# Rotary layers with one projection and an exchange of halves, and a first stage without added base rows

## What is computed

```python
for _ in range(3):
    prev = slots
    q = _ln(slots, lnq_g, lnq_b) @ wq + bq
    attn = softmax(k·q / scale, over the slots) + EPS_ATTN, each slot's share normalised over the tokens
    upd = jnp.einsum('bnk,bnd->bkd', attn, v)
    slots = upd @ wu + bu + prev
    h = _ln(slots, lnm_g, lnm_b) @ w1 + b1
    slots = gelu(h) @ w2 + b2 + slots
    slots = _ln(slots + x_cls[:, None, :], lnp_g, lnp_b)
```

```python
x1, x2 = (x[..., :half], x[..., half:])
return jnp.concatenate([x1 * cos - x2 * sin, x1 * sin + x2 * cos], axis=-1)
```

## Time and profile before

| | |
|---|---|
| median of three runs | 3954.4 us |
| the profiled execution, its own time | 3957.59 us |
| its span, first to last instruction | 3955.8 us |
| granted TensorE clock, mean | 0.963 |
| busy: TensorE, VectorE, ScalarE, GpSimd | 89%, 63%, 57%, 36% |
| stage "6", from the first context matmul at 2030.5 us to the end of its last layer and "7" | about 1925 us |

### The profile page before, as it was taken

One profiled execution on the slowest core, in us unless ns is written; L12 is line 12 of the kernel. 1 busy time (PEld: TensorE's weight loads), 2 busy tenths in 40 slices (PEclk: granted clock), 3 DMA queues, 4 the chain that ended last, 5 costly groups with the idle time before them and its releaser, 6 DMA issues.

```text
span 3955.8 us, 59358 instructions
## 1 busy us (share of the span) xinstructions
PE 3527.9 (89%) x23199; PEld 1634.4 (41%) x23199; DVE 2478.4 (63%) x4794; ACT 2263.7 (57%) x3266; POOL 1420.6 (36%) x1419
## 2 busy tenths in 40 slices
PE   6877999998899999989977898989999999989988
PEld 5667344443734444435551233333333333333334
DVE  6653544444365445534658787778877778778844
ACT  5524554553255555544314666677677777767784
POOL 5543433434244213420022243443443443443412
PEclk8889999999999999999987999999999999999998
DMA  3021100000210110011111011110110110110100
GB/s 124 12 69 56 50 17 23 6 17 25 78 40 23 28 34 6 23 46 35 33 44 49 11 47 28 44 50 26 44 50 26 44 50 26 52 42 26 41 12 17
DMA packets 139226, 146.05 MB, mean 37 GB/s; under 512 B 37241, under 2 KB 120649, under 8 KB 137238
## 3 DMA queue, kind: packets, MB, share of 16 engines
q1 hardware_dynamic: 135876, 135.96, 11.7%
q0 software_dynamic: 3072, 6.30, 0.5%
HBM read 69.00 MB, written 12.59 MB: 21 GB/s over the span
## 4 chain that ended last, share of the span: by engine, by line
PE 58%; DVE 24%; ACT 7%; POOL 6%; issue 3%; DMA 2%; SPq 1%; DVEq 0%; POOLq 0%; ACTq 0%
PE ps L1997 7%; PE ps L2013 6%; PE ps L2208 5%; DVE c1sm L2974 5%; DVE c0sm L2974 4%; PE ps L2125 3%; PE ps L2045 3%; PE ps L2194 2%; PE ps L2152 2%; PE ps L1938 2%; PE ps L2244 2%; PE ps L2252 2%; PE ps L1880 2%; ACT wA L2457 2%; PE ps L1870 2%
## 5 line engine op out<-in xcount | busy, mean ns | idle before, releaser
L2457 ACT ACTIVATE wA<-ps 128x1024 f32<-128x1024 f32 (+1 forms) x574 | 575.6, 1023 | 209.7 <-PE ps L2194 205.4
L2974 DVE TENSOR_REDUCE c0sm<-ps 128x2 f32<-128x1024 f32 x384 | 455.0, 1219 | 99.9 <-PE ps L2152 97.3
L2974 DVE TENSOR_REDUCE c1sm<-ps 128x2 f32<-128x1024 f32 x384 | 454.3, 1218 | 82.1 <-PE ps L2152 80.1
L2749 DVE TENSOR_REDUCE c1sm<-ps 128x2 f32<-128x1024 f32 x128 | 153.0, 1220 | 182.5 <-PE ps L1962 180.0
L2457 ACT ACTIVATE wB<-ps 128x1024 f32<-128x1024 f32 (+1 forms) x194 | 198.5, 1023 | 63.8 <-PE ps L2194 62.1
L2457 ACT ACTIVATE c0m<-ps 128x1024 f32<-128x1024 f32 (+1 forms) x192 | 196.2, 1022 | 59.0 <-PE ps L2194 57.3
L2749 DVE TENSOR_REDUCE c0sm<-ps 128x2 f32<-128x1024 f32 x128 | 151.9, 1219 | 93.9 <-PE ps L1962 92.3
L1734 PE MATMUL ps<-CST 128*128 128x256 bf16 x1330 | 190.4, 296 | 10.4 <-DMA CST<-in_cst 7.9
L3111 POOL TENSOR_SCALAR c0sm<-c0sm 128x4 f32<-128x4 f32 x40 | 7.8, 196 | 517.4 <-DVE c0sm L2529 517.0
L3111 POOL TENSOR_SCALAR c1sm<-c1sm 128x4 f32<-128x4 f32 x40 | 7.9, 196 | 509.8 <-DVE c1sm L2529 509.2
L2194 PE MATMUL ps<-c0ar 64*128 64x512 bf16 (+1 forms) x864 | 164.9, 388 | 25.2 <-DVE c1sm L2974 11.2
(11 more groups left out here) (980 smaller groups left out, 8366.6 us busy)
## 6 DMA issues: line engine op xcount, KB each, us to landing
c0ar<-c0m SPq DMA_DIRECT2D x216, 128.0 KB, 2.5
c1ar<-c0m SPq DMA_DIRECT2D x216, 128.0 KB, 2.4
c0m<-rscr SPq DMA_DIRECT2D x96, 128.0 KB, 3.0
c1m<-rscr SPq DMA_DIRECT2D x96, 128.0 KB, 3.0
wA<-in_x SPq DMA_DIRECT2D x1, 4112.0 KB, 21.6
wA<-in_x SPq DMA_DIRECT2D x1, 4096.0 KB, 12.9
wA<-in_lay SPq DMA_DIRECT2D x3, 1346.0 KB, 5.8
wB<-in_lay SPq DMA_DIRECT2D x3, 1346.0 KB, 5.8
```

The costliest lines, as they stand in the source:

```text
L2457: e.activation(P.ap[0:n, :, :], u.ap[0:n, :].rearrange("p (a q) -> p a q", a=2), ACT.Exp, scale=S8).then_inc(*A(("P8", n0, s, k), free=[u]))
L2749: e.tensor_reduce(c.sm[:, 2 * (g % 2), 2 * j:2 * j + 2], u.ap.rearrange("p (h k) -> p h k", h=2)[:, :, 0:n], AX, ALU.max, negate=True).the ...
L2974: e.tensor_reduce(c.mneg[:, j, :, s // 4, s % 4], u.ap.rearrange("p (a k) -> p a k", a=2), AX, ALU.max, negate=True).then_inc(*V(free=[u]))
```

## The change

The rotary weights are stored once. TensorE makes one projection into one bank, VectorE multiplies it by the cosine rows and by the sine rows (reading the same bank twice), and four DMAs of 32 partitions each exchange the halves of the sine product, since the halves of a head lie 32 partitions apart. GpSimd adds the exchanged product and goes on as before. A buffer `R` has 1536 columns in place of 1280, a layer's packed weights have 512 columns fewer.

In the first stage `s0base` is gone. The bias `bu` is added to the context's value rows once for each batch, before the rounds (the shares of a slot sum to one, so it comes out as a bias). `BC` is put into PSUM by an identity matmul ahead of the second one, and VectorE adds `y` itself.

The planner's constants and seeds of stages "0", "1", "2" and "6" are other ones; those of "3", "4" and "5" are the same. The costs in the requests follow the new steps.

```diff
-    "6": dict(lag=0.0744, weight=0.0116, even=0.0008, held=0.2624, table=1.1605, apart=55.0617, spread=0.0027, seed=2100, stagger=13.3148, ...
+    "6": dict(lag=0.0395, weight=0.0032, even=0.0016, held=0.2624, table=1.3751, apart=55.0617, spread=0, seed=7767, stagger=13.3148, ...
...
-        R6 = Bufs([carve(1280) for _ in range(3)])
+        R6 = Bufs([carve(1536) for _ in range(3)])
...
-                yield from do("s0base", c, ("base", k), w["bu"], chain=[("G", 1.3)], after=t)
...
-                yield from do("s0base", c, ("base2", k), BC[:, 128 * b:128 * b + 128], chain=[("G", 1.3)], after=ty)
...
-            (U, R), t = yield Want([("T", 1.92 * ncol / 512), ("V", 2.2 * ncol / 1024 + .12), ("G", 1.3)], [two, R6], t)
-            emit("rp", ch, n, ww, src, skey, ncol, U, R)
-            two.give(U, t[1])
-            t = t[2]
+            (U, R), t = yield Want([("T", 0.96 * ncol / 512), ("V", 2.2 * ncol / 1024 + .12)], [banks, R6], t)
+            emit("rp", n, ww, src, skey, ncol, U, R)
+            banks.give(U, t[1])
+            _, t = yield Want([("S", 1.3)], after=t[1])
+            emit("rx", ch, n, ncol, R)
+            _, t = yield Want([("G", 1.3)], after=t[0])
+            emit("rpa", ch, n, ncol, R)
+            t = t[0]
...
+            def rx(ch, n, ncol, R):
+                w.wait_ge(*V.at(("rp", n)))
+                for p in range(0, 128, 32):
+                    q = p ^ 32
+                    e.dma_start(R.ap[p:p + 32, 1024:1024 + ncol], R.ap[q:q + 32, 512:512 + ncol]).then_inc(*D("x" + ch)(("rx", n)))
...
-            def s0w2(c, k, h, u):
+            def s0w2(c, b, k, h, u):
+                w.wait_ge(*V.at("bc"))
+                for s in u.clear():
+                    w.wait_ge(*s)
+                e.matmul(u.ap, IDN, bc4(BC[:, 128 * b:128 * b + 128]), start=True, stop=False, skip_group_check=True)
                 w.wait_ge(*A.at(("s0h", k)))
-                for s in u.clear():
-                    w.wait_ge(*s)
                 for j in range(4):
-                    i = e.matmul(j4(u.ap, j), j4(h.ap, j), W0["w2"], start=True, stop=True)
+                    i = e.matmul(j4(u.ap, j), j4(h.ap, j), W0["w2"], start=False, stop=True, skip_group_check=True)
...
-                for k in range(2):
-                    i = e.matmul(U.ap[:, 512 * k:512 * k + ncol], j4(ww, k), src, start=True, stop=True)
-                i.then_inc(*T(("rp", n)))
+                e.matmul(U.ap[:, 0:ncol], ww, src, start=True, stop=True).then_inc(*T(("rp", n)))
...
-                w.wait_ge(*G.at(("base2", k)))
-                e.tensor_tensor(c.y, v4(u.ap), v4(c.ar[:, 1700:2212]), ALU.add).then_inc(*V(free=[u]))
+                w.wait_ge(*V.now())
+                e.tensor_tensor(c.y, v4(u.ap), c.y, ALU.add).then_inc(*V(free=[u]))
...
-                    e.tensor_tensor(o, v, CSIN, ALU.mult).then_inc(*V(("rp", n), free=[U]))
+                    e.tensor_tensor(o, bcg(U.ap, 2), CSIN, ALU.mult).then_inc(*V(("rp", n), free=[U]))
...
-            def rp(ch, n, ww, src, skey, ncol, U, R):
+            def rpa(ch, n, ncol, R):
                 o = R.ap
-                w.wait_ge(*V.at(("rp", n)))
-                e.tensor_tensor(o[:, 0:ncol], o[:, 0:ncol], o[:, 512:512 + ncol], ALU.add).then_inc(*G(("rp", n)))
+                w.wait_ge(*D("x" + ch).at(("rx", n)))
+                e.tensor_tensor(o[:, 0:ncol], o[:, 0:ncol], o[:, 1024:1024 + ncol], ALU.add).then_inc(*G(("rp", n)))
...
-LAY_COLS = [(n, 256) for n in ("q", "k", "cq", "ck")] + [(n, 128) for n in ("v", "so", "cv", "co")] + \
+LAY_COLS = [(n, 128) for n in ("q", "k", "cq", "ck", "v", "so", "cv", "co")] + \
```

More of the change, by code:

```diff
@@ L32 @@
     "5": dict(lag=0.0459, weight=0.0146, even=0.0061, held=0.012, table=3.6948, apart=0, spread=0.3107, seed=2311, bias=dict(G=0.872, TVA=-0.769, TAV=0.748, S=0.899, VG=-1.033, TV=0.596, T=1.359, V=-1.043, TA=0.476, TVAV=0.305, VTA=0.117), turns=(), shift=-24.819, keep=0.0),
-    "6": dict(lag=0.0744, weight=0.0116, even=0.0008, held=0.2624, table=1.1605, apart=55.0617, spread=0.0027, seed=2100, stagger=13.3148, bias=dict(T=0.244, S=0.373, VTA=-0.191, TVb=-0.054, A=-0.534, VG=-0.949, G=-0.49, TA=-0.046, TAb=-0.043, TAV=0.203, TVAV=0.587, TVV=0.107, V=0.182), turns=((13, 247, 0.3), (53, 150, 0.0), (379, 276, 0.3), (419, 456, 0.0), (3849, 853, 0), (3874, 642, 1.0), (4746, 100, 0), )),
+    "6": dict(lag=0.0395, weight=0.0032, even=0.0016, held=0.2624, table=1.3751, apart=55.0617, spread=0, seed=7767, stagger=13.3148, bias=dict(T=0.244, S=-0.259, VTA=-0.191, TVb=-0.054, A=-0.534, VG=-0.932, G=-0.369, TA=-0.046, TAb=-0.043, TAV=0.203, TVAV=0.253, TVV=0.107, V=-0.062, TVG=0.358, TVA=0.238), turns=((53, 150, 0.0), (419, 456, 0.0), )),
 }
@@ L733, in stage0 @@
                 c.zT.give(zt, t[0])
[L734 to L735 removed]
+                (u,), t = yield Want([("T", .95), ("V", .69)], [banks], t[1])
+                emit("s0w2", c, b, k, h, u)
                 banks.give(u, t[1])
@@ L1709, in store @@
                 e.dma_start(o[:, b], xb(b)).then_inc(*D("st_o")("o"))
-            run(dict(load=load, pre=pre, zl=zl, w1b=w1b, ysd=ysd, lay0=lay0, lay=lay, lay7=lay7, i6m=i6m, rd=rd, md=md, mw=mw, rq=rq, rw=rw, rb=rb, out=store))
+            run(dict(load=load, pre=pre, zl=zl, w1b=w1b, ysd=ysd, lay0=lay0, lay=lay, lay7=lay7, i6m=i6m, rx=rx, rd=rd, md=md, mw=mw, rq=rq, rw=rw, rb=rb, out=store))
             w.wait_ge(*D("st_o").at("o"))
@@ L2561, in s0c @@
                 e.memset(vw[:, 128:129], 1.0).then_inc(*V())
-                e.tensor_copy(vw[:, 0:128], u.ap[0:NCTX, 0:128]).then_inc(*V())
+                e.tensor_tensor(vw[:, 0:128], u.ap[0:NCTX, 0:128], W0["bu"][0:NCTX, :], ALU.add).then_inc(*V())
                 e.tensor_scalar(c.sm[0:NCTX, 0, 0:1], u.ap[0:NCTX, 128:129], S128, None, ALU.mult
@@ L2595, in s0u @@
                 r2 = c.sm[:, 6, 0:4]
-                base = v4(c.ar[:, 1700:2212])
-                w.wait_ge(*G.at(("base", k)))
+                w.wait_ge(*V.now())
                 for h, p in enumerate((u, u2)):
@@ L2605, in s0u, with s0w2 @@
                         i = e.scalar_tensor_tensor(out=c.y[:, q, :], in0=pv_[:, j, 0:128], scalar=r2[:, q:q + 1],
-                                                   in1=base[:, q, :], op0=ALU.mult, op1=ALU.add)
+                                                   in1=c.y[:, q, :], op0=ALU.mult, op1=ALU.add)
                     i.then_inc(*V(free=[p]))
-            def s0w2(c, k, h, u):
+            def s0w2(c, b, k, h, u):
                 w.wait_ge(*T.at(("s0w2", k)))
-                w.wait_ge(*G.at(("base2", k)))
-                e.tensor_tensor(c.y, v4(u.ap), v4(c.ar[:, 1700:2212]), ALU.add).then_inc(*V(free=[u]))
+                w.wait_ge(*V.now())
+                e.tensor_tensor(c.y, v4(u.ap), c.y, ALU.add).then_inc(*V(free=[u]))
             def xadd(c, b, dep=None):
@@ L3125, in lnb @@
                 e.tensor_tensor(c.ve, c.ve, c.rs, ALU.mult).then_inc(*G(("rs", n)))
-            def s0base(c, key, row):
-                base = v4(c.ar[:, 1700:2212])
-                w.wait_ge(*V.at("bc"))
-                e.tensor_tensor(base, c.y, bc4(row), ALU.add).then_inc(*G(key))
             def en(u):
@@ L3336, in arrays_of @@
     perm = np.array([(2 * s + p) * 8 + dd for p in range(2) for dd in range(8) for s in range(8)])
-    twin = np.array([(2 * s + p) * 8 + (dd + 4) % 8 for p in range(2) for dd in range(8) for s in range(8)])
     turn = np.array([(8 * q + 4 * y + i) * 8 + dd for q in range(2) for i in range(4) for y in range(2) for dd in range(8)])
-    both = lambda w: np.concatenate([w[:, perm], w[:, twin]], axis=1)
     lays = []
```

23 lines of the change are left out of this document (11 added, 12 removed).

## The result

The changed kernel takes 3950.7 us in the median of 19 runs (3937.2 to 3957.2), the kernel before 3958.4 us in 19 runs beside it. The ratio is 0.9979 with a 95% interval of 0.9970 to 0.9987. So it is faster by 0.2%, 8 us (5 to 12), where 28 us were forecast.

What follows compares the result with a forecast made beforehand. TensorE was taken to lead stage "6" at 91% busy, with VectorE a second limit close by. Terms -39 + 16 - 5 = -28 us gave 3929.6 us, stated as 3926 us against the median; range 3885 to 3968.

Steps and rivals of the forecast that it cites:

- more than a dozen exchanges: Sign of a wrong prediction: the chain shows more than a dozen exchanges; two to six were expected in stage "6"'s body.
- The rotary matmuls, -39: Stage "6", TensorE: one projection fewer per rotary step frees 65 us, of which 0.6 comes back, -39 us (0 to -65).
- VectorE's product, PSUM, buffers: Rotary step: product stays 1.225 us, at most +0.1 us each; PSUM gains; `G6` goes from seven buffers to eight, 0.
- rival D: VectorE's product becomes slower, say two passes of 0.7 us, or the clock falls in more stretches: 0 to +10 us; chance 0.04.
- The exchange, +16: Rotary steps of stage "6": four DMAs delay the sum 3.9 us, seen at start, end and two others: +16 us (+4 to +71).
- I let two of the ten stay open: Of ten rotary landings on stage "6"'s chain, filler covers all but two: +7.8 us.
- at nothing: SyncE's queue in stage "6": 312 more issues, some 156 us, cost nothing because the queue is mostly idle.
- Rival C: Stage "6": the exchange sets the pace; 11 open steps of 78 balance the gains, 18 give 3980 us; chance 0.17.
- Rival A: TensorE sets the pace, all freed time returns, only start and end show the exchange: -62, 3892 us; chance 0.15.
- Rival B: VectorE and PSUM take the place; freed time becomes waits for the row maxima: +3, 3957 us; chance 0.14.
- The first stage, -5: First stage: 24 GpSimd additions go, a quarter of them costing 0.8 us on the chain: -5 us (-12 to +5).
- The order, 0 within 12: New order of stages "0", "1", "2" and "6": no row prices it; taken as 0, with 12 us allowed either way.

Runs made afterwards that it cites:

- s0_only: The kernel before with the first stage of the change alone, without base rows and with new constants of stages 0, 1 and 2; ratio 0.9998 to before.
- twice_no_exchange: The changed kernel with the projection done twice and without the exchange, so rotary values differ from the reference; ratio 0.9991 to the kernel before.

## Why the prediction was right or wrong

The direction held, and the size didn't: -28 us forecast, -8 measured. One of the signs that I had named for a wrong prediction came: the chain shows more than a dozen exchanges, 23. And the stage isn't shorter by the 20 to 30 us that I expected to see.

**The rotary matmuls, -39.** It is 40 us in the old order, 55 in the new one without the exchange and 28 in the new one with it. So the share of the 65 us isn't a property of the work alone, and that my 0.6 hits the first of the three is in part luck. The records came as said, 156 with 85 us.

**VectorE's product, PSUM, buffers.** The product took 1.19 to 1.23 us, 1.21 in the median where it was 1.225, so the first half of rival D falls. Its second half, a lower clock in more stretches, did happen (0.96 and 0.98 where it was 1.00), but as a part of the exchange's price. No loss from `R` or `G6` shows; no run tried them alone.

**The exchange, +16. This is the step that failed.** An exchange that finds SyncE's queue free was priced well: 3.9 us taken, 3.9 the shortest of the 78, with issues of 0.59 in place of 0.5 us. The failed step is "I let two of the ten stay open". I counted the ten rotary landings that stood on the chain of before and let the plan fill most of them, which with start and end made four open delays. Taking the exchange away gives 51 us, worth 13 full delays of 3.9 us. The ten on the chain of before were not the only exposed ones: by the price, others must have been just beside it and joined when each got its delay (which ones, no run shows), and the filler that I took for granted, "four batches' worth", wasn't there to that extent. An order drawn without the exchange pays 257 us for it. The range's upper end for this term, 71 us, did hold the 51.

Two more steps of this term were wrong. I costed the new issues on SyncE's queue "at nothing", as the queue is mostly idle. It is (573 us of issues in stage "6"), but they come in bursts, and an exchange waits 1.1 us for its turn in the mean. And the sum adds -39 and +16 as if they were independent, where the measured pairs are -28 and +23 or -55 and +51. In either pair the exchange costs more than 16.

**Rival C, slower by the exchange, 0.17.** Its mechanism is the one that fits best: the delays appear in each batch's own run, with the exchange and the spreading on the chain. It named eleven open steps as the point of balance and over 13 as slower. By its own sum the 51 us are 13 steps of 3.9 us, so its count was about right and its gain too small, 59 in place of 44; its 18 steps and 3980 us didn't come. **Rival A** (all is given back) needs start and end as the only open exchanges, and falls; what it says of TensorE nearly holds without the exchange, 55 of the 65 us. **Rival B** (VectorE takes the place) falls too, since one projection less is worth 28 us even with the exchange there. The Trainium skill, "DMA: Bandwidth & Descriptors", section "Rules for kernel authors", says that split transfers serialise. Here the issues do, at 0.59 us each, while the fixed parts overlap: each of the four lands 2.0 us after its own issue in the median, and the last 3.9 us after the first issue. The estimate of 8 us made from the page was twice that. Whether one DMA for all 128 partitions would be quicker, as the page advises, no run tried.

**The first stage, -5.** `s0_only` gives -1 us, with an interval from -4 to +3, and the profiles a start of stage "6" that is 8 us sooner in the mean. The forecast lies between; it is neither borne out nor refuted.

**The order, 0 within 12.** `twice_no_exchange` puts it at -4 us together with the first stage and the single bank. Right, but not for the reason I gave: the 7 us between stretches say nothing of a new order, of which a nudge costs 33 us and foreign constants up to 290. It came out near 0 because both orders are fitted.

In one line, from before to after in the runs' ratios: the new order and first stage -4 us, one projection -55, the exchange +51, together -8. With the exchange put in first the same line reads -4, +23, -28.

## What to carry to other kernels

Work taken off the leading engine comes back in part, 28 to 55 of 65 us here, but a delay put into each stream's own run may cost as much, and the two costs don't simply add: measure them together and apart. Price such a delay by the number of its steps and their slack, not by those that stand on the chain today: the ones just beside it join as soon as it grows. And don't read the delay from one step: look at the whole set, and at what the issuing queue is doing when the step asks for it. In a kernel whose order is written out by a planner, compare versions only with constants fitted to each, mistrust differences smaller than a redraw, and keep the order fixed when a single operation is to be priced.

## What was not expected of the hardware

DMAs that no one waits for were nearly free: 312 more issues on SyncE's queue and their traffic moved the ratio by 0.0013, 5 us, within the noise. The same number of DMAs that are waited for stand in that queue behind each other, 1.1 us in the mean. Four 32-partition copies inside the chip's memory overlap their landings: each takes 2.0 us in the median, issued about 0.6 us apart. TensorE's granted clock falls where TensorE waits more: from 2400 to 2600 us it is 0.85 with the unplanned exchange (165 us busy in 200), 0.96 in the changed kernel (175) and 1.00 without the exchange (182). As worked out above, up to 21 of the exchange's 51 us may be work at the 1.2 GHz level; how much of that is real wasn't measured apart.
